# Inverse roots and a sigmoid rebuilt from logarithm and exponential in a one-core perceiver block, with a new order of steps

## What is computed

```
x = x + cross_attention(layernorm(x), ctx)       # 16 heads of 128
      q = rmsnorm(x Wq) gq ; k = rmsnorm(ctx Wk) gk ; softmax(q k / sqrt(128)) v Wo
x = x + self_attention(layernorm(x))             # 16 query and 4 key heads of 16, ternary weights
      q, k = rms_norm(q), rms_norm(k) ; rotary ; causal softmax ; rms_norm(y) w_proj
x = x + moe(layernorm(x))                        # top-1 of 8 experts, capacity 256, and a shared expert
      silu(x W1) * (x W3) W2
rmsnorm(v) = v * rsqrt(mean(v*v) + eps)          # one inverse root for each row and head
silu(v) = v * sigmoid(v)
```

## Time and profile before

| what | value |
|---|---|
| median of 3 runs | 1506.91 us (1506.75 to 1508.54) |
| the profiled execution's own time | 1508.46 us |
| its span, first to last instruction | 1506.6 us |
| mean granted TensorE clock | 0.933 |

### The profile page before, as it was taken

The page is one execution under the profiler, slowest core; times in us unless marked ns, Lnnn a source line. Parts: engine busy times, 40 slices in busy tenths (PEclk is TensorE's granted clock), DMA queues, the critical chain, the costliest instruction groups (busy, mean ns, idle before and its releaser), DMA issues.

```text
span 1506.6 us, 35628 instructions
## 1 busy us (share of the span) xinstructions
PE 1297.3 (86%) x10526; PEld 874.2 (58%) x10526; DVE 987.6 (66%) x3748; ACT 837.5 (56%) x3560; POOL 531.6 (35%) x1337
## 2 busy tenths in 40 slices
PE   5877898999999999989898989899999999955881
PEld 2554565666666666665656656566666666634661
DVE  6754777777677777776767676777767777732212
ACT  4445575747475757566566657575747575711110
POOL 2044152525252533435352515252535243310004
PEclk9998999999999999999999999999999999876996
DMA  9000010101010100000000000010101011002344
GB/s 370 31 23 15 9 30 11 32 11 32 11 32 11 33 11 29 11 26 18 22 21 22 21 8 29 11 32 11 32 11 32 11 32 39 31 3 75 120 153 126
DMA packets 41191, 59.65 MB, mean 40 GB/s; under 512 B 5094, under 2 KB 35953, under 8 KB 40096
## 3 DMA queue, kind: packets, MB, share of 16 engines
q1 hardware_dynamic: 36880, 50.73, 10.6%
q0 software_dynamic: 2064, 6.14, 1.2%
q10 hardware_dynamic: 2176, 2.10, 0.4%
HBM read 48.62 MB, written 10.49 MB: 39 GB/s over the span
## 4 chain that ended last, share of the span: by engine, by line
PE 49%; DVE 21%; issue 9%; POOL 8%; DMA 3%; ACT 3%; POOLq 0%; DVEq 0%; SPq 0%; ACTq 0%
PE AB L594 25%; PE Db L594 9%; PE Eb L594 5%; POOL prob L1177 4%; PE C L719 4%; PE C L594 3%; DVE kst L1312 3%; DVE rq L1360 2%; DMA ctxn<-expert_rows 2%; DVE nc_ L1284 2%; DVE nc_ L1285 2%; DVE nb_ L1286 1%; PE C L787 1%; DVE prob L1471 1%; PE C L734 1%
## 5 line engine op out<-in xcount | busy, mean ns | idle before, releaser
L950 ACT ACTIVATE AB<-AB 128x128 f32<-128x128 f32 (+1 forms) x1160 | 305.3, 263 | 172.8 <-PE AB L594 168.3
L1132 POOL TENSOR_TENSOR pjunk<-pjunk 128x1 f32<-128x1 f32 x288 | 56.1, 195 | 748.4 <-DVE sinv L1482 431.3
L1312 DVE BATCH_NORM_STATS2 kst<-AB 128x6 f32<-128x256 f32 x512 | 181.8, 417 | 68.1 <-PE AB L594 63.0
L950 ACT ACTIVATION_READ_ACCUMULATOR AB<-AB 128x1 f32 (+1 forms) x1160 | 217.3, 187 | 0.0
L594 PE MATMUL AB<-wk_hi,c_hi 128*128 128x512 f16 x512 | 203.7, 398 | 11.9 <-DVE smax L1471 2.9
L594 PE MATMUL AB<-wk_lo,c_hi 128*128 128x512 f16 x512 | 201.3, 393 | 0.0
L594 PE MATMUL AB<-wk_hi,c_lo 128*128 128x512 f16 x512 | 199.7, 390 | 0.0
L1020 ACT ACTIVATE prob<-prob,nbias,rq 128x257 f32<-128x257 f32 x256 | 150.6, 592 | 7.9 <-DVE nbias L1477 7.9
L1177 POOL TENSOR_SCALAR prob<-prob,sinv 128x257 f32<-128x257 f32 x256 | 123.4, 482 | 20.2
L594 PE MATMUL AB<-ctxT,qpT 128*128 128x257 f32 x512 | 124.0, 385 | 0.0
L594 PEld LDWEIGHTS AB<-wk_hi,c_hi 128*128 128x128 f16 x512 | 52.2, 102 | 94.7 <-issue 25.2
(11 more groups left out here) (252 smaller groups left out, 2923.8 us busy)
## 6 DMA issues: line engine op xcount, KB each, us to landing
ctxT<-in_ctxT SPq DMA_DIRECT2D x64, 128.5 KB, 2.1
ctxn<-in_ctxn SPq DMA_DIRECT2D x64, 128.0 KB, 2.1
wq_hi<-in_w SPq DMA_DIRECT2D x4, 768.0 KB, 5.0
wq_lo<-in_w SPq DMA_DIRECT2D x4, 768.0 KB, 6.3
expert_rows<-base POOLq DMA_DIRECT2D x1, 2048.0 KB, 15.5
xin<-in_x SPq DMA_DIRECT2D x16, 128.0 KB, 2.2
prob<-in_wqT SPq DMA_DIRECT2D x1, 2048.0 KB, 20.4
xres<-in_x SPq DMA_DIRECT2D x16, 128.0 KB, 2.0
```

What stands on the lines that cost most here:

```text
L950: ins = nc.scalar.activation(k, k, ACT.Square, accum_out=sums[0:m, h:h + 1])
L1132: own.mark(pool.tensor_tensor(pjunk[:, 0:1], pjunk[:, 1:2], pjunk[:, 1:2], ALU.mult))
L1312: ins = V.bn_stats(stats[:, 0, 2 * half + n], AB[0:m, 2 + half, 2 * D * n:2 * D * (n + 1)])
```

## The change

1. The guess of an inverse root comes from ACT: `Ln` of the mean square, then `Exp` with scale -0.5, which gives (mean square)^(-1/2). DVE refines it with one round of three instructions (`refined`) in place of ten. That holds for KN0, KN1, RQ and qkv; only the root of the last keys in the prologue (KNL) keeps `newton`. Each of the four steps on DVE is cut in two: KN0 and kn0, KN1 and kn1, RQ and rq, qkv and qr; between them stands ACT's gKN0, gKN1, gRQ, gqkv.
2. The sigmoid is three activations that wait for one another, exp(-ln(1 + exp(-x))), in place of one `Tanh`; DVE then multiplies twice (tensor_tensor) in place of two scalar_tensor_tensor.
3. ACT's first instruction loads a named table set; the orders of all four engines are changed.

```diff
 ORDER = {
-    "PE": """K0 pt3 K1 X K2 o3 K3 f Q xt1 rk0 qkv K4 QP s0 qk sc rk1 K5 K6 K7 pv pt0 s1 st pr rk2 s2 o0 xt2 rk3
+    "PE": """K0 pt3 K1 X K2 o3 K3 f Q xt1 K4 qkv QP rk0 s0 qk sc rk1 K5 K6 K7 pt0 pv s1 st pr rk2 s2 o0 xt2 rk3
               lg up s3 pt1 dn pos o1 pt2 o2""".split(),
-    "ACT": """K0 tl3 K1 X ph3 K2 oh3 K3 Q xt1 rk0 qkv K4 QP qk e0 K5 sc K6 K7 rk1 pv tl0 ph0 rk2 e1 oh0 xt2 rk3 up
-              e2 lg ph1 tl1 e3 oh1 ph2 tl2 oh2""".split(),
-    "DVE": """K0 X K1 XL dp3 K2 do3 K3 KN0 f Q RQ K4 qkv s0 sc i0 K5 sm K6 K7 KN1 ys dp0 yv s1 pr ln2 i1 s2 lg do0
-              up s3 i2 dp1 dn pos do1 dp2 i3 do2""".split(),
-    "POOL": """h0 n3 h3 h1 X c0 cl r1 h2 ln1 c3 r0 n0 c2 r2 c1 y r3 ln2 n1 n2 scat""".split(),
+    "ACT": """K0 tl3 K1 X ph3 K2 oh3 K3 gKN0 Q xt1 gRQ K4 qkv gqkv QP rk0 qk e0 rk1 K5 sc K6 K7 ph0 gKN1 pv tl0
+              rk2 e1 xt2 rk3 oh0 up e2 ph1 lg tl1 e3 oh1 ph2 tl2 oh2""".split(),
+    "DVE": """K0 X K1 XL dp3 K2 K3 KN0 do3 kn0 f Q RQ K4 rq qkv qr s0 sc K5 i0 sm K6 K7 KN1 dp0 kn1 ys yv s1 pr
+              ln2 i1 s2 do0 lg up s3 i2 dn dp1 pos do1 dp2 i3 do2""".split(),
+    "POOL": """h0 n3 h1 X h2 c0 c1 r0 cl ln1 r1 h3 n0 r2 y r3 ln2 c2 n1 c3 n2 scat""".split(),
 }
...
         def _(act):
+            nc.scalar.preload_act_table_set("natural_log_exp_and_others")
...
+            def sigmoid(p, k, out, x):
+                nc.scalar.activation(out, x, ACT.Exp, scale=-1.0).then_inc(sig_exp.sem, 1)
+                act.wait_ge(sig_exp.sem, sig_exp.at(p, f"e{k}"))
+                nc.scalar.activation(out, out, ACT.Ln, bias=1.0).then_inc(sig_exp.sem, 1)
+                act.wait_ge(sig_exp.sem, sig_exp.at(p, f"l{k}"))
+                return nc.scalar.activation(out, out, ACT.Exp, scale=-1.0)
...
+            def root_guess(p, name):
+                act.wait_ge(squares_ready.sem, squares_ready.at(p, name))
+                nc.scalar.activation(guess[name][:], squares[name][:], ACT.Ln).then_inc(log_ready.sem, 1)
+                act.wait_ge(log_ready.sem, log_ready.at(p, f"g{name}"))
+                nc.scalar.activation(guess[name][:], guess[name][:], ACT.Exp, scale=-0.5).then_inc(guess_ready.sem, 1)
...
+            def refined(p, name, out):
+                w, c = guess[name][:], nc_[:, 0:guess[name].shape[1]]
+                dve.wait_ge(guess_ready.sem, guess_ready.at(p, f"g{name}"))
+                step(V.scalar_tensor_tensor(c, w, -0.5, w, ALU.mult, ALU.mult))
+                step(V.tensor_tensor(c, c, squares[name][:], ALU.mult))
+                return V.scalar_tensor_tensor(out, c, 1.5, w, ALU.add, ALU.mult)
...
             def step_up(p):
-                dve.wait_ge(sig_tanh.sem, sig_tanh.at(p, "h"))
-                V.scalar_tensor_tensor(all_of(hT[:]), all_of(sig[:]), 1.0, C[:, 0, 0:FC * P], ALU.add, ALU.mult)\
+                dve.wait_ge(sig_ready.sem, sig_ready.at(p, "h"))
+                V.tensor_tensor(all_of(hT[:]), C[:, 0, 0:FC * P], all_of(sig[:]), ALU.mult).then_inc(drained["4"].sem, 1)
```

More of the change, by code:

```diff
@@ L162 @@
               pt2 o2""".split(),
[L163 to L166, removed]
+    "ACT": """KL K0 wq0 K1 wq1 K2 X K3 gKN0 rkl Q W0a W0b W1a W1b K4 gRQ QP M0a M0b K5 M1a M1b tw rk0 e0 rk1 e1 K6 ph0 tl0 K7 gKN1 ph1 tl1 oh0 rk2 e2 rk3 oh1 e3 ph2 tl2 oh2""".split(),
+    "DVE": """low wk KL KNL K0 K1 X K2 XL wql K3 gg KN0 kn0 Q W0l wt0 W1l K4 RQ rq wt1 M01 wt K5 M23 tw s0 s1 i0 K6 dp0 i1 K7 KN1 kn1 do0 dp1 s2 s3 i2 dp2 do1 i3 do2""".split(),
     "POOL": """hl h1 h3 h2 h0 rkl X r0 r1 cl c0 n0 c1 n1 r2 c2 r3 n2 c3""".split(),
@@ L328, in build @@
         nb_ = sb("nb_", [P, NB * H])
+        squares = {n: sb(f"squares_{n}", [P, k]) for n, k in (("KN0", NB * H), ("KN1", NB * H), ("RQ", H), ("qkv", NQK))}
+        guess = {n: sb(f"guess_{n}", [P, k]) for n, k in (("KN0", NB * H), ("KN1", NB * H), ("RQ", H), ("qkv", NQK))}
         nc_ = sb("nc_", [P, NB * H])
@@ L381, in build @@
                              full=entries("POOL", FULL, "h"))
-        rk_ready = Events(sem("rk_ready"), pro=steps_among("DVE", PRO, ["KNL", "KN0", "KN1"]),
-                          full=steps_among("DVE", FULL, ["KN0", "KN1"]))
+        rk_ready = Events(sem("rk_ready"), pro=steps_among("DVE", PRO, ["KNL", "kn0", "kn1"]),
+                          full=steps_among("DVE", FULL, ["kn0", "kn1"]))
         rq_ready = Events(sem("rq_ready"), **fills)
+        chains = ["KN0", "KN1", "RQ", "qkv"]
+        squares_ready = Events(sem("squares_ready"), pro=steps_among("DVE", PRO, chains), full=steps_among("DVE", FULL, chains),
+                               last=["qkv"])
+        guesses = ["gKN0", "gKN1", "gRQ", "gqkv"]
+        log_ready = Events(sem("log_ready"), pro=steps_among("ACT", PRO, guesses), full=steps_among("ACT", FULL, guesses),
+                           last=["gqkv"])
+        guess_ready = Events(sem("guess_ready"), pro=steps_among("ACT", PRO, guesses), full=steps_among("ACT", FULL, guesses),
+                             last=["gqkv"])
         high_steps = ["wq0", "wq1", "W0a", "W0b", "W1a", "W1b", "M0a", "M0b", "M1a", "M1b", "X"]
@@ L1326, in key_norms @@
                 sums_from_stats(m, stats, n // H, src)
[L1327 to L1328 removed]
+                if event == "KNL":
+                    step(V.tensor_scalar(na[0:m, 0:n], src, 1.0 / (D * WK_SCALE ** 2), X_EPS, ALU.mult, ALU.add))
+                    newton(n, out, m).then_inc(rk_ready.sem, 1)
+                else:
+                    V.tensor_scalar(squares[event][:], src, 1.0 / (D * WK_SCALE ** 2), X_EPS, ALU.mult, ALU.add)\
+                        .then_inc(squares_ready.sem, 1)
             def step_K(p, j):
@@ L1510, in step_qkv, with step_qr @@
                 step(V.tensor_reduce(qkn[:], qk2[:].rearrange("p (h n) -> p h n", n=AD), AX.X, ALU.add))
-                step(V.tensor_scalar(na[:, 0:NQK], qkn[:], 1.0 / AD, A_EPS, ALU.mult, ALU.add))
-                step(newton(NQK, qki[:]))
+                V.tensor_scalar(squares["qkv"][:], qkn[:], 1.0 / AD, A_EPS, ALU.mult, ALU.add).then_inc(squares_ready.sem, 1)
+            def step_qr(p):
+                step(refined(p, "qkv", qki[:]))
                 step(V.tensor_tensor(qki[:, 0:AH], qki[:, 0:AH], again[:], ALU.mult))
```

46 lines of the change are left out of this document (23 added, 23 removed).

## The result

The changed kernel takes 1457.98 us (median of 4 runs, 1456.99 to 1459.04); the kernel before, run on the same chip, 1506.83 (1506.39 to 1508.54). The ratio is 0.967, 95% interval 0.966 to 0.969: 49 us less. Forecast were 1489 us, with a range of 1462 to 1507.

The account below looks back on a forecast made before the run. PE was taken to bound the loop, with 5.5 us of gaps a period. 1.7 + 0.4 - 1.0 = 1.1 us, times 15, plus 1.4 at the ends, gave 18 us off: 1489 us, range 1462 to 1507.

Parts of the forecast that it names:

- A: Two roots ahead of heads on DVE: shorter chain shrinks PE's 2.1 us gap; gain 1.7 us a period, bounds 0.8 and 2.1.
- D: PE's granted clock, falling to 0.5 after the wait for heads: taken as 0 a period, bounds -1.5 and +1.1 us.
- B: pt0's transposes ahead of pv on PE fill the wait for K7's statistics: gain 0.4 us a period, bounds 0 and 1.05.
- C: Longer sigmoid and reordered period end delay slot_s, K0 and pt3: cost 1.0 us a period, bounds 0 and 2.45.
- The pauses of 0.65 and 0.6 us: DVE idling in the chain to heads: 0.65 us for K4's statistics, 0.6 us for ACT's guess of qkv.
- rival 1: PE's clock stays high after the shorter gap ahead of qk: another 1.5 us a period, 1467 us; chance 0.18.
- The ends: Prologue and last tile, outside the 15 periods: about 1 us and 0.4 us gained, 1.4 together.
- Rival 2: The gap only moves: ACT's in-order queue delays QP's copies and s0; 1507 us, no change; chance 0.12.
- Rival 3: Slower: sigmoid and reordering reach slot_s in full, scatter to K0 costs 2.45 us a period; 1512 us; chance 0.15.
- Rival 4: A table is loaded around each Ln on ACT, 12.8 us of ACT a period; over 1600 us; chance 0.03.

Follow-up runs that it names:

- dp1_first: Changed kernel with dp1 ahead of dn in DVE's order, as it stood before, nothing else; 1436.73 us, ratio 0.954.
- fill_gap: Kernel before, with nine unread 128x512 products on PE ahead of the wait for heads in each full period; 1490.31 us, ratio 0.988.
- delay: Changed kernel with ten dependent 128x20 copies on DVE behind the wait for the q and k root's guess, each full period; 1517.60 us, ratio 1.009.
- fill_sc: Changed kernel with four unread 128x512 products on PE ahead of step sc's wait for ACT's copy of heads; 1449.55 us, ratio 0.960.
- sigmoid_only: Kernel before, with the new sigmoid alone (three activations, two DVE products without constants); 1510.55 us, ratio 1.003.
- functions_alone: Kernel before, its order of steps kept, with ACT's guesses plus one refining round and the new sigmoid; 1592.04 us, ratio 1.056.
- tanh_after: Changed kernel with the sigmoid by tanh as before, one activation and DVE's two products with constants; 1554.71 us, ratio 1.031.
- both_early: Changed kernel with dp1 ahead of dn on DVE and POOL's split h0 of the next period ahead of the scatter; 1436.47 us, ratio 0.954.

## Why the prediction was right in direction and wrong in size

Means over 14 periods, from the starts and ends of the named steps in both traces:

| stretch | term | forecast, us | measured, us | before, after |
|---|---|---|---|---|
| x_hi to the end of heads | A | -1.7 | -2.05 | 31.19, 29.14 |
| heads to sc, sc to K7's end | D | 0 | -0.19 - 1.27 = -1.46 | 2.54 + 12.40, 2.35 + 11.13 |
| K7's end to s1 | B | -0.4 | -0.45 | 2.84, 2.39 |
| s1 to st | | 0 | -0.04 | 2.36, 2.32 |
| st to the next x_hi | C | +1.0 | +0.84 | 28.16, 29.00 |
| sum | | -1.1 | -3.16 | 79.49, 76.33 |

**A** held. The pauses of 0.65 and 0.6 us were measured at 0.68 and 0.54. It came out 0.35 larger, the bound of 2.1 just enclosing it. About 0.1 of this is the choice of pattern: from Q's sums to the end of `heads` DVE took 13.16 us there, the shortest of the 14, whose mean is 13.25. The rest was not followed up.

**B** held to 0.05 us. **C** held in its sum and in its places, the waits of 0.73 at K0 and 0.38 at pt3. Its split was wrong: I had the sigmoid delay s3 by 0.4 to 0.5, and dp1_first got all of C back with the sigmoid in place.

**D failed**, and it is the step that put the result outside the range. "[...] the gap ahead of sc stays, and dense matmuls now begin sooner behind it, so a low stretch would lie on more work. I take 0, bounds -1.5 and +1.1." It was worth -1.46 us a period; over the 15 periods of the sum that is 22 of the 31 us that were missed. The term's own bound of -1.5 would have held it; the range did not reach so far. Nor does the range follow from its words: rival 1 with B at its bound is 1467 less 15 x 0.65, some 1457, and not 1462. The rows already hinted at the price: the earlier trace rows show the same stretch 1.1 us apart for clock alone, both being periods in which it fell, so what no fall at all would give had to be larger, and no row showed it. I read 0 out of a mechanism that I could argue both ways. fill_gap and delay settle it: with the gap filled and `heads` unmoved 16 us come back; with the gap put back into the changed kernel its clock falls in all 14 periods again, and 1.88 us of PE's time a period go with it.

**The ends** hardly differ from the sum. Counted as the sum counts, 15 periods of 3.16 us are 47.3 of the 49.6 between the profiled executions, so the ends gave 2.3 us where I had 1.4. What of this is the change stays open, since the stretch ahead of the second `x_hi` scatters by more. It ends at 131.7 us in the changed kernel, but at 133.8 in delay, 134.0 in fill_sc and 131.6 in dp1_first, whose prologues are the same code; the kernel before has 135.4, fill_gap with the same prologue 135.2, and sigmoid_only, whose prologue has the new set loaded but the old roots, 133.8. Within one code the scatter of 2.4 us goes with the clock: in this stretch it is at 0.5 for 20.5 us in the changed kernel and in dp1_first, for 23.9 in delay and fill_sc, and for 27.3 in the kernel before and fill_gap. The clock is not all of it, as sigmoid_only has 27.3 too.

**The rivals.** Rival 1, the clock stays high, with 0.18, is in the main what happened, though five of 14 periods still have a short fall. Its 1.5 us a period was nearly the measured 1.46; its 1467 is still 9 us above the result, since A gave more and C cost less. Rival 2 did not happen, but functions_alone shows what ACT's order can pass on when K4 stands behind gqkv. Rival 3 did not: K0 waits 0.73 us, far from 2.45. (Its sum is 1 us too high: 15 x 0.35 less the 1.4 of the ends is 4 us, 1511.) Rival 4's loads did not come in the changed kernel, but did in tanh_after, which keeps tanh beside the guesses; there 176 us of loads came with a kernel 97 us slower, some half of the 192 us behind that rival's "over 1600".

## What to carry to other kernels

A gap on PE had two prices here: its own length, and what the matmuls behind it cost at 1.2 GHz (2.1 and 1.9 us a period in delay). Before taking 0 for the clock, count PE's busy time over equal instructions in stretches with and without a fall, and put that into the range whenever a change shrinks or opens a gap of a microsecond or two. A cheaper function paid only once its steps found room on the engine that takes them, so run the order and the function apart: each alone was slower here than the kernel before, and the best single edit, dp1_first, came from asking what the changed order made late.

## What the runs showed that I had not expected

- A delay of 2.2 us on DVE cost 4.0 us a period, 1.9 of them through PE's clock (delay), and 2 us of useless matmuls in each period made the kernel 16 us faster (fill_gap). The Trainium skill (TensorE: Matmul & The Clock Gate, "What's actually happening") says that the half-rate clock is the default and activity lifts it; products that nobody reads lifting it agree with that.
- Falls hang on more than the nearest gap: filling the 1.12 us ahead of sc ended them (fill_sc), but so did taking away 0.7 us at K0, some 40 us ahead of the place where the clock used to fall, with the gap ahead of sc in place (dp1_first). Whether the wait at K0 itself acts over such a distance, or the shorter period that comes with it (75.03 us in place of 75.85), was not tried; both_early has neither the wait nor the longer period, and its clock fell once. It stays open.
- One tanh in the loop brought 137 table loads of 1.28 us in place of one (tanh_after), nearly all of them ahead of the Ln or the Exp of a guess.
